# Attention projection of unit u − 2 in four 32-column tiles in front of the sums of unit u, both in one pair of PSUM banks

## What is computed

```python
cp = leaky_relu(representations @ Wc.T + bc)
q, k, v = ...                                   # 16 heads: dh = 8, dv = 64
scores = einsum('bqhd,bkhd->bhqk', q, k) / SCALE
attn = softmax(scores, axis=-1)
out = einsum('bhqk,bkhd->bqhd', attn, v).reshape(B, T, 1024)
proj = leaky_relu(out @ Wo.T + bo)
return representations + proj
```

## Time and profile before

| | |
|---|---|
| median of 3 runs | 1030.12 us (1028.76 to 1032.16) |
| profiled execution, its own time | 1030.25 us |
| its span, first to last instruction | 1028.4 us |
| mean granted TensorE clock | 0.957 |
| TensorE busy | 924.7 us, 90% |
| VectorE busy | 772.9 us, 75% |
| GpSimd busy | 631.9 us, 61% |
| ScalarE busy | 546.9 us, 53% |

### The profile page before, as it was taken

How to read it: one execution, slowest core, us unless ns; L and a number is a source line. 1 busy time by engine, 2 the same in 40 slices (tenths; PEclk the granted TensorE clock), 3 DMA queues, 4 the chain that set the end, 5 groups by cost and what they waited for, 6 DMA issues and landing times.

```text
span 1028.4 us, 20166 instructions
## 1 busy us (share of the span) xinstructions
PE 924.7 (90%) x7292; PEld 479.5 (47%) x7298; DVE 772.9 (75%) x1300; ACT 546.9 (53%) x927; POOL 631.9 (61%) x555
## 2 busy tenths in 40 slices
PE   5899998999999999999989997799967675789997
PEld 3346563233333333333323334789956332358795
DVE  5864777888888888887888825875599999995513
ACT  1574445666666666666656784353455032257363
POOL 5470425788678667876877883023567878773412
PEclk9999998999999999999999998899998888699999
DMA  9353424111011201011101123467830200235462
GB/s 318 137 184 119 143 73 145 32 50 46 23 52 29 56 23 49 29 55 55 36 24 46 38 70 109 150 205 222 275 116 11 69 23 21 76 106 151 147 195 68
DMA packets 92273, 96.99 MB, mean 94 GB/s; under 512 B 23184, under 2 KB 68624, under 8 KB 91920
## 3 DMA queue, kind: packets, MB, share of 16 engines
q1 hardware_dynamic: 87056, 85.21, 26.9%
q0 software_dynamic: 5120, 10.50, 3.3%
HBM read 70.43 MB, written 24.77 MB: 93 GB/s over the span
## 4 chain that ended last, share of the span: by engine, by line
PE 75%; DVE 13%; POOL 6%; issue 3%; DMA 2%; ACT 1%; SPq 0%; ACTq 0%; DVEq 0%; POOLq 0%
PE ps L255 71%; PE ps L258 4%; POOL ar L261 3%; DVE small L274 2%; DVE ar L261 2%; DVE ar L274 2%; DVE osb L274 1%; POOL psum_sb L261 1%; DVE acc_sb L261 1%; DVE ps L261 1%; DMA psum_sb<-in_L_bv 1%; DVE psum_sb L261 1%; POOL acc_sb L320 0%; POOL gT L320 0%; SPq L301 0%
## 5 line engine op out<-in xcount | busy, mean ns | idle before, releaser
L255 PE MATMUL ps<-ar 64*64 64x512 bf16 (+4 forms) x5312 | 545.4, 449 | 33.3 <-DVE ar L261 11.6
L255 PEld LDWEIGHTS ps<-ar 64*64 64x64 bf16 (+2 forms) x5312 | 273.3, 139 | 284.2 <-issue 88.3
L298 ACT ACTIVATE ar<-ps 128x1024 f32<-128x1024 f32 (+2 forms) x336 | 303.7, 908 | 160.0 <-PE ps L255 154.4
L274 DVE TENSOR_REDUCE small<-ps 128x2 f32<-128x1024 f32 (+2 forms) x276 | 306.9, 1138 | 45.7 <-PE ps L255 44.3
L261 POOL TENSOR_TENSOR psum_sb<-psum_sb,ar 128x1024 f32<-128x1024 f32 x91 | 214.9, 2361 | 48.7 <-DVE on_sb L261 38.5
L261 POOL TENSOR_TENSOR ar<-ar 128x512 f32<-128x512 f32 (+1 forms) x80 | 106.4, 1334 | 36.5 <-DVE ar L274 17.3
L320 POOL DMA_INDIRECT gT<-ysort,rt x48 | 46.0, 959 | 95.6 <-issue 94.6
L261 DVE TENSOR_TENSOR ar<-ps,ar 128x256 f32<-128x256 f32 (+4 forms) x56 | 56.4, 1011 | 50.2 <-PE ps L255 41.9
L261 POOL TENSOR_TENSOR psum_sb<-ar 128x1024 f32<-128x1024 f32 x32 | 75.7, 2367 | 29.3 <-ACT ar L298 25.2
L295 ACT COPY ar<-ps 128x256 f32<-128x256 f32 (+1 forms) x84 | 30.6, 383 | 86.7 <-PE ps L255 54.3
L255 PE MATMUL ps<-wA,xnT 128*128 128x512 f32 (+3 forms) x192 | 67.3, 465 | 7.4 <-DVE ar L261 3.8
(11 more groups left out here) (159 smaller groups left out, 1040.9 us busy)
## 6 DMA issues: line engine op xcount, KB each, us to landing
ar<-in_L_up SPq DMA_DIRECT2D x48, 384.0 KB, 4.0
ar<-in_L_b SPq DMA_DIRECT2D x32, 322.0 KB, 3.6
rec_sb<-lscr SPq DMA_DIRECT2D x64, 128.0 KB
scr<-ar SPq DMA_DIRECT2D x48, 128.0 KB, 2.0
ar<-xsort SPq DMA_DIRECT2D x40, 128.0 KB, 2.6
ysort<-ar SPq DMA_DIRECT2D x40, 128.0 KB, 3.6
ar<-scr SPq DMA_DIRECT2D x32, 112.0 KB
xsort<-xs SPq DMA_DIRECT2D x12, 256.0 KB, 6.9
```

Of the source, the lines that this page charges most:

```text
L255: return self.e.matmul(o, l, r, start=start, stop=stop) if self.e else Nothing()
L274: return self.e.tensor_reduce(o, a, AX.X, op, negate=True) if negate else self.e.tensor_reduce(o, a, AX.X, op)
L298: return self.e.activation(o, a, fn, **kw) if self.e else Nothing()
```

## The change

Three things change, all in the first attention.

The projection of unit `u` goes from `k = 12` to `k = 17` (`proj_step`), that is to step 1 of unit `u + 3`, the step in which the sums of unit `u + 2` are made, in front of them. Only the last two units of each batch row (14, 15, 30, 31) keep `k = 12`. It becomes four matmuls of 32 output columns, each in its own column tile. `island(u)` takes one pair of banks for both and waits for both banks: the projection fills the first, the sums the second. VectorE's addition to `acc_sb` follows to the same step, behind its half of `osb`.

The row transpose becomes two of 64 rows each, in 64x64 tiles and two banks, and ScalarE copies both at once. Since two banks of a pair now have owners of their own, scores and max pairs wait for both.

```diff
+    def proj_step(u):
+
+        return 17 if u % 16 < 14 else 12
...
     def tensor_program(pe):
         ring = [(4, 5, 6, 7)]
+        islands = {}
+
+        def island(u):
+
+            if u not in islands:
+                islands[u] = take(ring[0])
+                pe.wait_ge(*vacant(islands[u]))
+                pe.wait_ge(*vacant(islands[u] + 1))
+            return islands[u]
...
-            for b in banks:
+            for b in banks if len(banks) > 1 else (banks[0], banks[0] + 1):
                 pe.wait_ge(*vacant(b))
...
-            pe.tr(pb[0:48, 0:128], nsp[:, 48 * k:48 * k + 48], identb).then_inc(*filled(b, ("rowsT", B)))
+            if B == 0:
+                pe.tr(pb[0:48, 0:128], nsp[:, 0:48], identb).then_inc(*filled(b, ("rowsT", B)))
+                return
+            pe.wait_ge(*vacant(b + 1))
+            for n in range(2):
+                r = slice(64 * n, 64 * n + 64)
+                ins = pe.tr(ps[:, b + n, :].bitcast(BF16)[0:48, 0:64], nsp[r, 48 * k:48 * k + 48], identb[r, r])
+            ins.then_inc(*filled(b, ("rowsT", B)))
...
             if k == 1:
-                b = take(ring[0])
-                pe.wait_ge(*vacant(b))
+                b = island(u) + 1
                 pe.wait_ge(*at("exp", 8 * u + 7))
...
-            if k == 12:
+            if k == proj_step(u):
                 pi = 2 * (g % 4) + pr
-                b = take(ring[0])
+                b = island(u + 2) if proj_step(u) == 17 else take(ring[0])
                 pe.wait_ge(*vacant(b))
                 pe.wait_ge(*at("scaled", u))
                 if u == 0:
                     pe.wait_ge(*at("wb0_in", 0))
-                pe.mm(ps[:, b, :], wA[:, 1280 + 128 * pi:1408 + 128 * pi],
-                      on_sb[:, 512 * (u % 2):512 * (u % 2) + 512]).then_inc(*filled(b, ("proj", u)))
+                for r in range(0, 128, 32):
+                    ins = pe.mm(ps[r:r + 32, b, :], wA[:, 1280 + 128 * pi + r:1312 + 128 * pi + r],
+                                on_sb[:, 512 * (u % 2):512 * (u % 2) + 512])
+                ins.then_inc(*filled(b, ("proj", u)))
 
         def tails(x):
+            unit_tail(x // 8 - 3, x % 8 + 16)
             unit_tail(x // 8 - 1, x % 8)
             unit_tail(x // 8 - 2, x % 8 + 8)
...
                 pe.wait_ge(*vacant(b0))
+                pe.wait_ge(*vacant(b0 + 1))
```

More of the change, by code:

```diff
@@ L1811, in max_rows @@
                 act.wait_ge(*at("rows1_in", B - 2))
-            pb = ps[:, bank["rowsT", B], :].bitcast(BF16)
-            act.acp(mT[:, 128 * k:128 * k + 128], pb[0:48, 0:128]).then_inc(*emptied(("rowsT", B), ("rows", B)))
+            b, dst = bank["rowsT", B], mT[:, 128 * k:128 * k + 128]
+            if B == 0:
+                ins = act.acp(dst, ps[:, b, :].bitcast(BF16)[0:48, 0:128])
+            else:
+                ins = act.acp(v3(dst, 64), ps[0:48, b:b + 2, :].bitcast(BF16)[:, :, 0:64])
+            ins.then_inc(*emptied(("rowsT", B), ("rows", B)))
         def max0():
```

## The result

The changed kernel takes 1021.64 us (median of 5 runs, 1020.90 to 1022.63), the kernel before beside it 1029.01 (5 runs, 1028.44 to 1032.16). The ratio is 0.9923, interval 0.9906 to 0.994: 7.4 us less, against 10.2 forecast, and 1.7 us above the predicted 1019.9.

What follows compares the result with a forecast made beforehand. TensorE was taken as the bound, busy 924.7 of 1028.4 us. Terms: 5.3 (13 long units), 4.35 less 0.3 (short), 0.25 (units 14, 15), 0.6 (ranks), together 10.2 us, giving 1019.9 us; range 1015 to 1026.

Steps and rivals of the forecast that it cites:

- A round costs what the sums' rounds cost: Tiled projection beside the sums: two added rounds at 0.43, 0.86 us for 1.15, so 0.29 less per unit.
- The long unit exceeds the short one: Units with the row transpose wait for VectorE's reduction, not `acc_sb`: 0.51 over units without it, not 0.63; 0.12 less.
- The transpose's form: Row transpose in two 64x64 tiles: costs between nothing and 0.17 us, either covered by the wait for VectorE.
- the addition behind the halves: VectorE's `acc_sb` addition, 0.70 us, moved behind `osb`: costs nothing, since VectorE is idle there for 1.11 us.
- Weight loads in the open: Rival: projection rounds cost 0.53 each, 0.2 more in 28 units, 5.8 us, time 1025.7; chance 0.10.
- The long unit's whole wait: Rival: units with the row transpose lose all their wait, 0.45 more in 13 units, time 1014.1; chance 0.08.
- the tiles stream together: Projection's four tiles run at once; the rival, one after another, 64 us more, time 1094, had chance 0.03.
- the ranks: Unit at 527.63 to 546.66: scores 1.07 us earlier, 0.66 more than a long unit gains; 0.6 taken.
- 15 short ones × 0.29 = 4.35, less 0.3 for units 28 and 29: Short units' part of the sum; 0.3 taken off because sum 31 hangs on the `lscr` DMA and GpSimd.
- as long as the others' slack holds: Condition in the attention's units for each TensorE nanosecond taken out to be a nanosecond of the span.
- Given back: Rival: GpSimd's or a DMA's chain, or the clock, holds TensorE at 409 to 486, ranks or end; 1028, chance 0.07.
- the thirteen units: Attention window from 198.58 to 381.12 us, TensorE nearly always busy; the prediction's terms make it 4.5 us shorter.

Runs made afterwards that it cites:

- experiment 2: The changed kernel with the projection as one 128x128 matmul again, at its new place directly in front of the sums; 1027.60 us, ratio 0.9971.
- experiment 3: The changed kernel with the row transpose in one piece again, 128x48 as before; 1021.98 us, ratio 0.9915.
- experiments 6 and 7: The changed kernel with the projection of units 25 and up back at `k = 12`, tiled; 1103.18 us (0.9935) on a slower chip, then 1022.57 us (0.9928).
- set three: Third set of four kernels, run where the kernel before takes 1029.95 us (28 runs).
- experiments 9 and 12: The changed kernel with unit 27's `psum_sb` addition on GpSimd, 1024.87 us; the same with the scaling into `on_sb` also at `k = 9`, 1027.61 us.
- 4 and 8: The changed kernel with `acc_sb`'s addition one step later in units 26 to 29, 1021.86 us; with unit 27's `psum_sb` addition on GpSimd, 1098.97 us.
- set two: Second set of four kernels, on a chip where the program takes 8% longer (kernel before: 1109.62 us, 31 runs).

## Why the prediction was right, and where it was not

*Right, by the mechanism forecast.* A round costs what the sums' rounds cost: two rounds take 0.89 to the sums against 0.86 taken, 0.29 less per short unit, 0.30 measured. The long unit exceeds the short one by 0.52 (0.51 forecast), held by VectorE's reduction of the step before; the chain's row names it, and experiment 2 gets it from the move alone. The transpose's form and the addition behind the halves cost nothing (experiment 3, the 1.38 of idle).

*The rivals.* Weight loads in the open would have made rounds of 0.53 and short units of 13.66, which is what the untiled projection of experiment 2 has (13.65). In tiles the rounds are 0.46 and 0.43 apart, although all four tiles share the rows of the array; by the rule that I had put beside this rival from the Trainium skill, "TensorE: Matmul & The Clock Gate", Part 3, The mechanism, loads for the same rows would not overlap, and these rows leave at most 0.03 for that. The full-width pass takes 0.53 again in experiment 2. My reason for it, weights that go into the same tile, holds for the column tiles as well, so it does not explain the difference, and no run does. (28 × 0.2 is 5.6 and not the 5.8 put down, which makes this rival's time 1025.5.) The long unit's whole wait did not go, and the tiles stream together.

*Mis-sized: the ranks, 0.6 more than a long unit.* The scores behind the ranks do come 1.17 earlier (533.17 − 522.28 = 10.89 from the unit's start, 12.06 before), but I compared that with a long unit's gain and left out that the projection now follows it in the same unit, 0.86 to 0.89. Net about 0.3, and 0.25 measured at equal clock, where the term made it 1.0. The clock, which I had left as it was, did not fall in the profiled execution, and its 1.65 covered this.

*Wrong: units 26 and up.* "15 short ones × 0.29 = 4.35, less 0.3 for units 28 and 29" and 0.41 for unit 27 made 1.6 us from unit 26 to the end of attention; it came to a loss of 1.0. The step that failed is the rule that a TensorE nanosecond taken out is a nanosecond of the span "as long as the others' slack holds". I tested that slack at unit 9 (0.32, and it did cost: 0.16) but not from unit 27 on, where VectorE's addition makes VectorE's queue wait for GpSimd. There the moved projection stands behind the wait: experiments 6 and 7 give unit 27 back 0.9, and in set three GpSimd's queue takes it again from unit 28 on. "Given back", which had these places in it, was right in kind for 2.6 of the 10 us.

*Missed by 0.7: the thirteen units.* 0.50 of it is unit 3 (14.54, where 14.45 − 0.41 = 14.04 was due): its scaling already ran into GpSimd's addition before, and now does so for longer, 1.26 in place of 0.94. 0.15 is unit 9.

What stays open: why the part behind the attention, with no changed instruction, takes anything from 375.4 to 379.1 us in these executions (the first piece, 8.33 to 9.87, is only a part of it), and with it most of the losses of experiments 9 and 12. The granted clock goes with it, but not strictly: at a mean of 0.92 there it takes 375.4 to 377.9, at 0.91 or 0.90 it takes 376.5 to 379.1, and a hundredth of 377 us is 3.8 us. What makes the clock differ isn't shown. No version here beats the changed kernel clear of the noise; experiments 3, 4 and 8 (in set two) have ratios of 0.9911 to 0.9915, inside its interval. The scaling at `k = 9` from unit 26 on alone, where it gave the five units 62.88 us against 64.56, was not run.

## What to carry to other kernels

Put matmuls of the same tile shape next to each other: entering and leaving a tiling (here 0.53 from start to start in place of 0.43) is then paid once. Moving and reshaping together gave 7.4 us here, and either alone 2.1. Before counting a step moved off the middle of a unit as a gain, look in every stage, not only in the common unit, at what frees the bank that it will take; behind a cross-engine wait it adds its whole length. When a small VectorE instruction with two SBUF inputs is moved, check what GpSimd does at that moment.

## What the hardware showed that I had not expected

- VectorE's 0.68 us instruction with both inputs in SBUF takes up to 2.77 us beside a GpSimd addition, and ends 0.54 to 0.57 us after it; one with an input in PSUM stays at 0.68.
- The second pass of a full-width f32 matmul starts 0.53 us behind the first, in four 32-column tiles 0.46, and 0.43 where the same tiling continues.
- Behind the same 2.6 us of idle the granted clock of TensorE fell to 0.91 in the mean of the unit in one execution and stayed at 1.00 in another of the same instructions, 1.65 us apart.
